# Two small fp32 matmuls per image, each issued as two over the left and right 64 columns

## The chip, the cores and the metric

The kernel runs on one core of one Trainium2 chip. The metric is the device time of one execution in microseconds (us), as the median of several executions. TensorE appears in the profile as two rows: PE for the matmuls and PEld for the loads of their stationary operand (the weights). DVE is VectorE, ACT is ScalarE, POOL is GpSimd, SP is the engine that issues most of the transfers.

## The reference

The input x has 16 images of 32 channels and 96 x 96 pixels. Each channel of each image is normalised (mean 0, variance 1 over its pixels) to v. The means of v over the pixels go through a small gate of seven outputs and a softmax. Each image then gets its own two 3 x 3 kernels as a mixture of seven experts:

```
pooled = v.mean(axis=(-2, -1))
gate   = softmax(pooled @ gate_w.T + gate_b)
kw1    = einsum('be,eoihw->boihw', gate, experts_w1) + conv1_w      # kw2 and both biases alike
out    = x + v + conv(relu(conv(v, kw1) + kb1), kw2) + kb2
```

All of it is fp32. The small matmuls on the way to the gate are fp32 in the kernel as well.

## The kernel before

**Tiling.** An image lies on all 128 partitions: partition group g (of G = 4, 32 channels each) holds the rows 4b + g, in NB = 24 blocks b. A convolution is a sum of matmuls with 128 rows (4 image rows x 32 channels) and 64 columns (2 output rows x 32 channels). It comes in two sides: one fills PSUM partitions 0 to 63 and the other 64 to 127, each through its own half of the array's columns. One side reads the image tile (a1, a2), the other a copy in which the partition halves are swapped (c1, c2). fp32 accuracy comes from fp16 pairs: three products (high x high, high x low, low x high), each over three horizontal taps. So one group (5 blocks, 480 pixels) is 9 pairs of matmuls, and there are GRP = 5 groups for each of the two convolutions of an image: `products` (L369), which records all 2880 convolution matmuls at line 375.

**The two small matmuls.** `gather_rows` (L355) sums the statistics of the four partition groups: a 128 x 128 matrix `same` times a 128 x 12 tile `triples`, into PSUM `pstat`. `logits` (L362) sums over all partitions with a 128 x 128 matrix of ones times the 128 x 7 tile `gwp`, into `pgate`. Each is one fp32 matmul in the code. In the profile each of them stands as two LDWEIGHTS and two MATMUL, since fp32 is executed in two passes.

**Order of the work.** Nothing is planned at run time: each engine has its own list, written out by hand in a function `slot(s)`, one slot for each image, inside a loop of six slots that runs twice (`schedule`, L235). The slots of the engines are coupled by semaphores.
- PE, slot s: conv1 of image s, groups 0 to 3; `gather_rows` of image s+2; conv1 group 4; conv2 of image s-1, groups 0 and 1; `logits` of image s+2; conv2 groups 2 to 4 (L449 to L461). conv1 group 0 waits for the weights, for the low part of the image, for the crossed copy c1 (a transfer) and for PSUM bank 0, which `finish` of image s-2 frees.
- DVE, slot s: `finish` group 4 of image s-2 (L683, adds the result to the image, out of PSUM), `statistics` (L591), the low parts of the hidden layer (L669), `channel_moments` of image s+2 (L610), which waits for `gather_rows`, seven steps of `mixture` for the weights of image s+1 (L638), `weights` (L658), `finish` groups 0 and 1 of image s-1, `softmax_in` of image s+2 (L621), which waits for `logits`, then `finish` groups 2 and 3.
- POOL: `coefficients` (L836, follows channel_moments), the low part of the next images (L852), the residual (L868).
- ACT: normalisation, the hidden layer out of PSUM (L521), the crossed copy for conv2 (L538).
- SP, slot s: load of image s+2 (four transfers, L273), the crossed copy c1 of image s (two transfers, L300), then the stores of image s-2: four transfers after `finish` group 2 and four after `finish` group 4 (L287). These are in one queue and are issued in this order.

Of the kernel before, what the change touches and what calls it, by code (L numbers as in the profile page):

```python
# [35 lines left out]
P = 128  # L36
# [54 lines left out]
def build(nc, x, w1, b1, w2, b2, ew1, eb1, ew2, eb2, gw, gb, out):  # L91
    N, C, H, W = x.shape
    E = ew1.shape[0]
    G = P // C
# [15 lines left out]
    with ctx:  # L110
        def sb(name, shape, dt=F32):
            return ctx.enter_context(nc.sbuf_tensor(name, shape, dt))

        def sem(name):
            return ctx.enter_context(nc.semaphore(name))
# [21 lines left out]
        same = sb("same", [P, P])  # L137
        row = sb("row", [P, 2, G])
        triples = [sb(f"triples{i}", [P, G, 3]) for i in range(2)]
        ones = sb("ones", [P, P])  # L140
# [8 lines left out]
        gwp = [sb(f"gwp{i}", [P, E]) for i in range(RING)]  # L149
# [6 lines left out]
        pstat = ctx.enter_context(nc.psum_tensor("pstat", [P, 512], F32))  # L156
        pgate = ctx.enter_context(nc.psum_tensor("pgate", [P, 512], F32))
# [21 lines left out]
        rows_ps = sem("rows_ps")  # L179
# [6 lines left out]
        gate_ps = sem("gate_ps")  # L186
# [132 lines left out]
        def _(pe):  # L319
# [35 lines left out]
            def gather_rows(t):  # L355

                pe.wait_ge(mv_ok, t.number + 1)
                nc.tensor.matmul(pstat[:, 0:3 * G], same[:, :],  # L358
                                 triples[t.parity][:, :, :].rearrange("p g a -> p (g a)"),
                                 start=True, stop=True).then_inc(rows_ps, 1)  # L360

            def logits(t):  # L362
                pe.wait_ge(gwp_ok, t.number + 1)
                if not t.known(0):
                    pe.wait_ge(logit_ok, t.number)
                nc.tensor.matmul(pgate[:, 0:E], ones[:, :], gwp[t.ring][:, :],
                                 start=True, stop=True).then_inc(gate_ps, 1)

            def products(v, s, g, pairs, *sides):  # L369
                for image, weight in pairs:  # L370
# [62 lines left out]
            for n in range(8):  # L433
                transpose_kernels(n)
            gather_rows(Sample(0, 0))
            transpose_table()
            logits(Sample(0, 0))
            gather_rows(Sample(0, 1))
            logits(Sample(0, 1))
            warm_up()  # L440
            first_conv1()
            conv1_group(Sample(0, 1), 0)
            gather_rows(Sample(0, 2))
            conv1_group(Sample(0, 1), 1)
            conv1_group(Sample(0, 1), 2)
            conv1_group(Sample(0, 1), 3)
            logits(Sample(0, 2))

            def slot(s):  # L449
# [462 lines left out]
```

## Time and profile before

| | us |
|---|---|
| median of 3 runs | 372.83 |
| lowest, highest | 371.85, 376.41 |
| time of the profiled execution | 373.65 |
| its span, first to last instruction | 371.8 |
| PE busy | 320.5 (86%) |
| DVE busy | 301.0 (81%) |
| ACT busy | 252.6 (68%) |
| POOL busy | 199.6 (54%) |

The span is that of the profiled execution; the 1.85 us between it and the time lie outside the first and last instruction. A busy PE is not PE at its peak, since the matmuls overlap: a matmul of the convolution lasts 0.37 us in the record, but two sides run at once and a new pair starts every 0.20 us. The mean granted TensorE clock was 0.97 of full speed. DMA moved 58.19 MB, mean 157 GB/s.

### The profile page before, as it was taken

The page shows a single profiled execution, that of the slowest core. Times are in us where ns is not written, and L with a number is a line of the kernel's source. Part 1 is how long each engine was busy: PE and PEld are TensorE (multiplying, and loading weights), DVE is VectorE, ACT ScalarE, POOL GpSimd, SP SyncE. Part 2 cuts the span into 40 slices and gives each one's busy share as a digit, 9 for nine tenths or more (in the row PEclk, how much of TensorE's full clock was granted, in tenths as well). Part 3 has the DMA queues.
Part 4 walks back from the last instruction along what each step waited for, and adds up shares of the span by engine and source line. Part 5 has one row for each costly group of instructions (what it writes and reads, how often), then busy time and mean ns, then how long its engine had stood idle before and what let it go on. Part 6 is the DMA issues. An engine that isn't in the chain of part 4 may idle for free.

```text
span 371.8 us, 8541 instructions
## 1 busy us (share of the span) xinstructions
PE 320.5 (86%) x2983; PEld 198.4 (53%) x2983; DVE 301.0 (81%) x679; ACT 252.6 (68%) x278; POOL 199.6 (54%) x236
## 2 busy tenths in 40 slices
PE   2328773599999997999997999989999999999994
PEld 2216532356465754565554557555556555676552
DVE  3699945699979998899988799998999898796432
ACT  1155229877877887797877578887778787866720
POOL 8039417492928484666648084847576674933000
PEclk9999968599999999999999899999999999999999
DMA  9942990607989596949795795969697967194055
GB/s 194 219 74 56 229 189 2 130 3 189 198 191 194 136 234 151 219 116 220 168 203 127 175 194 150 220 150 230 147 203 165 213 148 178 42 216 112 18 130 127
DMA packets 107148, 58.19 MB, mean 157 GB/s; under 512 B 102497, under 2 KB 103009, under 8 KB 107105
## 3 DMA queue, kind: packets, MB, share of 16 engines
q1 hardware_dynamic: 106304, 57.03, 72.3%
q10 hardware_dynamic: 608, 0.59, 0.6%
q8 instruction: 26, 0.43, 0.5%
q14 instruction: 18, 0.14, 0.1%
q0 software_dynamic: 192, 0.01, 0.0%
HBM read 19.47 MB, written 18.87 MB: 103 GB/s over the span
## 4 chain that ended last, share of the span: by engine, by line
PE 38%; DVE 26%; DMA 11%; issue 9%; SPq 9%; ACT 3%; POOL 2%; ACTq 0%; DVEq 0%; POOLq 0%
PE pg L375 36%; DMA c<-a 10%; DVE mix L645 6%; DVE a L672 5%; DVE img L688 4%; SPq L273 4%; SPq L287 3%; DVE wts L662 3%; DVE stats L600 2%; SPq L300 2%; PE pg L338 2%; POOL a L858 1%; DMA natural<-in_L_conv_conv_w 1%; PE pstat L358 1%; DVE wts L665 1%
## 5 line engine op out<-in xcount | busy, mean ns | idle before, releaser
L375 PE MATMUL pg<-a,wts 128*64 128x480 f16 (+1 forms) x1440 | 295.2, 364 | 15.1 <-DMA c<-a 9.2
L375 PE MATMUL pg<-c,wts 128*64 128x480 f16 (+1 forms) x1440 | 300.7, 369 | 0.0
L375 PEld LDWEIGHTS pg<-c,wts 128*64 128x64 f16 x1440 | 155.3, 110 | 72.6 <-issue 1.1
L375 PEld LDWEIGHTS pg<-a,wts 128*64 128x64 f16 x1440 | 155.8, 110 | 52.1 <-issue 15.3
L858 POOL TENSOR_TENSOR a<-xh,a 128x576 f16<-128x576 f32 x64 | 85.3, 1364 | 12.9 <-POOL col L866 8.5
L533 ACT ACTIVATE hid<-pg,col 128x480 f32<-128x480 f32 x80 | 52.4, 656 | 40.8 <-PE pg L375 26.1
L549 ACT COPY c<-a 64x2352 f32<-64x2352 f32 x32 | 68.9, 2153 | 16.3 <-DVE a L672 13.2
L645 DVE SCALAR_TENSOR_TENSOR mix<-bank,gate,mix 128x386 f32<-128x386 f32 x96 | 74.0, 771 | 2.4
L839 POOL TENSOR_TENSOR col<-col,minus_half 128x1 f32<-128x1 f32 x16 | 13.5, 845 | 113.6 <-DVE col L618 113.6
L672 DVE TENSOR_TENSOR a<-hid,a 128x480 f16<-128x480 f32 x80 | 55.5, 695 | 20.8 <-ACT a L533 19.1
L872 POOL TENSOR_SCALAR img<-img,col 128x1152 f32<-128x1152 f32 x32 | 58.4, 1834 | 0.1
L688 DVE SCALAR_TENSOR_TENSOR img<-pg,img 128x480 f32<-128x480 f32 (+1 forms) x80 | 47.1, 631 | 12.7 <-PE pg L375 10.2
L533 ACT ACTIVATE a<-pg,col 128x480 f16<-128x480 f32 x80 | 52.6, 657 | 0.0
L600 DVE BATCH_NORM_STATS2 stats<-img 128x6 f32<-128x384 f32 x96 | 45.6, 544 | 0.1
L490 ACT ACTIVATE xh<-img,col 128x2304 f32<-128x2304 f32 x16 | 36.9, 2306 | 10.0 <-POOL col L840 10.0
L495 ACT ACTIVATE a<-img,col 128x2304 f16<-128x2304 f32 (+1 forms) x17 | 37.3, 2194 | 6.5 <-POOL col L840 6.5
L662 DVE TENSOR_TENSOR wts<-mix,wts 128x384 f16<-128x384 f32 x16 | 20.6, 1290 | 0.3 <-ACT wts L518 0.3
L358 PE MATMUL pstat<-triples,same 128*128 128x12 f32 x32 | 6.9, 290 | 15.4 <-DVE triples L607 15.4
L518 ACT CAST wts<-mix 128x384 f16<-128x384 f32 x16 | 8.2, 512 | 16.0 <-DVE mix L645 16.0
L358 PEld LDWEIGHTS pstat<-triples,same 128*128 128x128 f32 x32 | 5.4, 211 | 21.4 <-DVE triples L607 16.0
L665 DVE COPY wts<-wts 64x768 f16<-64x768 f16 x32 | 13.2, 414 | 0.8
L615 DVE COPY col<-pstat 128x1 f32<-128x1 f32 x16 | 2.5, 157 | 13.3 <-PE pstat L358 13.0
(61 smaller groups left out, 146.0 us busy)
## 6 DMA issues: line engine op xcount, KB each, us to landing
c<-a SPq DMA_DIRECT2D x28, 588.0 KB, 8.7
img<-in_x SPq DMA_DIRECT2D x56, 288.0 KB, 5.6
out<-img SPq DMA_DIRECT2D x60, 180.0 KB, 3.0
out<-img SPq DMA_DIRECT2D x60, 108.0 KB, 2.4
c<-a SPq DMA_DIRECT2D x8, 294.0 KB, 5.3
img<-in_x SPq DMA_DIRECT2D x16, 144.0 KB, 5.0
out<-img SPq DMA_DIRECT2D x4, 120.0 KB, 2.1
out<-img SPq DMA_DIRECT2D x8, 60.0 KB, 1.8
```

The source lines that it names most:

```text
L375: last = nc.tensor.matmul(pg[g][side * 64:side * 64 + 64, at:at + nb * W].rearrange("p (b w) -> p b w", w=W), wts[s.c % WSETS][kind][:, v, ...
L490: nc.scalar.activation(xh[t.parity][:, :, :], img[t.ring][:, :, :], ACT.Identity, bias=c[:, NBIAS:NBIAS + 1], scale=c[:, RSTD:RSTD + 1]).t ...
L495: return nc.scalar.activation(a1[t.parity][:, HI, b0:b1, 1:1 + W], img[t.ring][:, b0:b1, :], ACT.Identity, bias=c[:, NBIAS:NBIAS + 1], sca ...
L533: last = nc.scalar.activation(o, pg[g][:, 0:SPG * W].rearrange("p (b w) -> p b w", w=W), ACT.Relu, bias=c[:, B1:B1 + 1], scale=HS / WS)
L549: last = nc.scalar.copy(d, a[:, :, first:first + NB * RP // 2])
L600: last = nc.vector.bn_stats(stats[t.ring][:, j, :], flat[:, j * SC:(j + 1) * SC])
L645: nc.vector.scalar_tensor_tensor(out=mix[:, (e + 1) % 2, :, :], in0=bank[:, e, :, :], scalar=gate[t.ring][:, e:e + 1], in1=bank[:, E, :, : ...
L662: link(nc.vector.tensor_tensor(st[:, :, LO, :], mix[:, E % 2, :, 0:TAPS], st[:, :, HI, :], ALU.subtract))
L672: nc.vector.tensor_tensor(a2[s.parity][:, LO, j0:j1, 1:1 + W], hid[g_parity(s, g)][:, :, :], a2[s.parity][:, HI, j0:j1, 1:1 + W], ALU.subt ...
L688: nc.vector.scalar_tensor_tensor(out=r, in0=pg[g][:, 0:(b1 - b0) * W].rearrange("p (b w) -> p b w", w=W), scalar=1.0 / (WS * HS), in1=r, o ...
L858: last = nc.gpsimd.tensor_tensor(a1[t.parity][:, LO, b0:b1, 1:1 + W], xh[t.parity][:, b0:b1, :], a1[t.parity][:, HI, b0:b1, 1:1 + W], ALU. ...
L872: last = nc.gpsimd.tensor_scalar(img[t.ring][:, b0:b1, :], img[t.ring][:, b0:b1, :], c[:, RS1:RS1 + 1], c[:, RB:RB + 1], ALU.mult, ALU.add)
```

## The change

`gather_rows` and `logits` are each issued as two matmuls: one over columns 0 to 63 of the stationary matrix, writing PSUM partitions 0 to 63, and one over columns 64 to 127, writing partitions 64 to 127. The moving operand, all 128 rows of it, is read by both. The semaphore is raised by the second one alone. The values computed are the same, and nothing else changes.

```diff
             def gather_rows(t):
 
                 pe.wait_ge(mv_ok, t.number + 1)
-                nc.tensor.matmul(pstat[:, 0:3 * G], same[:, :],
-                                 triples[t.parity][:, :, :].rearrange("p g a -> p (g a)"),
-                                 start=True, stop=True).then_inc(rows_ps, 1)
+                for h0, h1 in ((0, P // 2), (P // 2, P)):
+                    last = nc.tensor.matmul(pstat[h0:h1, 0:3 * G], same[:, h0:h1],
+                                            triples[t.parity][:, :, :].rearrange("p g a -> p (g a)"),
+                                            start=True, stop=True)
+                last.then_inc(rows_ps, 1)
 
             def logits(t):
                 pe.wait_ge(gwp_ok, t.number + 1)
                 if not t.known(0):
                     pe.wait_ge(logit_ok, t.number)
-                nc.tensor.matmul(pgate[:, 0:E], ones[:, :], gwp[t.ring][:, :],
-                                 start=True, stop=True).then_inc(gate_ps, 1)
+                for h0, h1 in ((0, P // 2), (P // 2, P)):
+                    last = nc.tensor.matmul(pgate[h0:h1, 0:E], ones[:, h0:h1], gwp[t.ring][:, :],
+                                            start=True, stop=True)
+                last.then_inc(gate_ps, 1)
```

## Rows read from the trace of the kernel before

**Rows 1.** The page: granted clock in 40 slices, and the busy line.
```profile
PEclk9999968599999999999999899999999999999999
PE 320.5 (86%) x2983; PEld 198.4 (53%) x2983; DVE 301.0 (81%) x679; ACT 252.6 (68%) x278; POOL 199.6 (54%) x236
```
**Rows 2.** Stretches by PE slot: length, busy by engine, clock, DMA share, GB/s.
```profile
82.44:103.13 20.69, 19.05 (x189) 11.86 (x183) 19.84 (x48) 17.45 (x19) 13.04 (x15) 1.00 0.82 175
103.13:122.03 18.90, 18.90 (x184) 11.78 (x186) 16.35 (x39) 14.05 (x17) 10.59 (x12) 1.00 0.88 189
122.03:143.26 21.23, 19.05 (x189) 11.88 (x184) 20.33 (x46) 17.82 (x19) 14.61 (x16) 1.00 0.82 177
143.26:162.16 18.90, 18.90 (x185) 11.24 (x186) 15.62 (x38) 13.36 (x17) 9.90 (x12) 1.00 0.85 182
...
244.18:263.62 19.44, 19.06 (x184) 11.16 (x185) 17.17 (x41) 14.89 (x18) 11.43 (x14) 1.00 0.86 185
...
302.77:321.67 18.90, 18.90 (x184) 11.29 (x186) 17.14 (x41) 14.88 (x17) 11.40 (x13) 1.00 0.56 127
321.67:339.64 17.97, 17.97 (x187) 14.07 (x183) 14.49 (x28) 12.34 (x17) 9.61 (x8) 1.00 0.59 136
```
**Rows 3.** Who waited for whom, 82 to 303 us: total, times, longest.
```profile
DVE col L615 <- PE pstat L358: 7.0, 7, 1.2
PE pg L375 <- DVE img L688: 5.5, 4, 2.3
PE pg L375 <- DMA c<-a: 3.9, 4, 2.2
```
**Rows 4.** Chain of waits, 103 to 144 us: start, us, what.
```profile
103.13 7.53 PE pg L375 x71
110.66 0.34 PE pstat L358 x2
...
111.02 0.06 DVE col L615
...
122.01 0.58 DVE img L688
...
122.61 0.04 SPq L287
...
131.03 1.02 SPq L300
...
132.11 10.81 DMA c<-a
142.92 0.34 issue
143.26 0.80 PE pg L375 x6
```
**Rows 5.** PE in order of time around one `logits`: start, us, operation.
```profile
236.84 0.37 PE L375 MATMUL pg<-c,wts 128*64 128x480 f16 x1
...
237.04 0.36 PE L375 MATMUL pg<-c,wts 128*64 128x480 f16 x1
237.05 0.36 PE L375 MATMUL pg<-a,wts 128*64 128x480 f16 x1
237.34 0.39 PE L366 MATMUL pgate<-gwp,ones 128*128 128x7 f32 x2
237.66 0.39 PE L375 MATMUL pg<-c,wts 128*64 128x480 f16 x1
...
237.89 0.37 PE L375 MATMUL pg<-c,wts 128*64 128x480 f16 x1
```
**Rows 6.** The same stretch, the weight loads.
```profile
237.34 0.30 PEld L366 LDWEIGHTS pgate<-gwp,ones 128*128 128x128 f32 x2 [0.39 <-issue]
237.69 0.11 PEld L375 LDWEIGHTS pg<-c,wts 128*64 128x64 f16 x1
```
**Rows 7.** Line 358 after 100 us: ns minimum, median, maximum.
```profile
L358 PEld LDWEIGHTS pstat<-triples,same x22: 186/188/189, 110.6 to 310.3; 128*128 128x128 f32 x22
L358 PE MATMUL pstat<-triples,same x22: 259/270/280, 110.6 to 310.4; 128*128 128x12 f32 x22
```
**Rows 8.** PE in order of time in the first 25 us.
```profile
18.61 0.60 PE L358 MATMUL pstat<-triples,same 128*128 128x12 f32 x2 [4.29 <-DVE triples L607]
23.91 0.60 PE L358 MATMUL pstat<-triples,same 128*128 128x12 f32 x2 [1.62 <-DVE triples L607]
```

## The prediction

> **What bounds the kernel now.** I read the page first. PE is busy for 86% and DVE for 81% of the span, and the granted clock is near full speed in nearly all slices [rows 1]: neither engine is bound on its own, so the order of waits decides. Next I cut the trace at the starts of conv1 group 0, which gives stretches of one PE slot [rows 2]. The shortest slots take 18.90 us with PE busy for all of it. The slot from 321.67 us on, in which neither `gather_rows` nor `logits` runs any more, takes 17.97 us. So the two small matmuls cost PE (18.90 - 17.97) = 0.93 us a slot, 0.46 us each. From 82.44 to 302.77 us there are 11 slots, from the first row to the one at 302.77 [rows 2], 20.03 us on average, 1.13 us more than PE needs: PE-bound slots alternate with slots of up to 21.23 us. The waits say what fills the rest [rows 3]: PE waits 9.4 us in all at group 0 of conv1, in eight slots, and DVE waits 7.0 us for the result of `gather_rows`. The wait put down to DVE's `finish` is doubtful, as other semaphores are tested with it.
>
> The chain of waits shows the cycle [rows 4]. Conv1 groups 0 to 3 start at 103.13 us and take 7.53. `gather_rows` follows, and DVE has it at 111.02. DVE then works to the end of `finish` group 2 at 122.59 (11.57 us). SP then issues eight stores, four loads and the two crossing transfers, until the last one leaves at 132.11 (9.5 us). It lands 10.81 us later, and conv1 group 0 starts at 143.26. That is 40.1 us for **two** slots: 7.53 + 0.36 + 11.57 + 9.5 + 10.81 + 0.34. An image's crossing goes back to the `gather_rows` of two slots before. Two such chains run side by side, one a slot behind the other, and the slot between (122.03 us) starts when PE gets there. So PE's own time per slot counts only where no landing holds it, and on the chain itself stands one `gather_rows` per two slots, and no `logits`.
>
> **What one site costs.** Around a `logits` [rows 5] pairs start every 0.20 us (236.84, 237.04). The first pass of the small matmul starts 0.30 us after the last pair, the next pair 0.62 us after it, and the one after that another 0.23 later. Without the site 0.20 would stand between them, so the site costs 0.42 + 0.03 = 0.45, which agrees with the 0.46 above. Its parts: the weight loads of the two passes end 0.30 after the first begins, and one lasts 0.188 in the record [rows 6, 7], so they begin 0.30 - 0.19 = 0.11 apart. That makes about 0.21 of serial loading of 128 columns. Ahead of it lies 0.30 - 0.20 = 0.10, in which nothing streams. Behind it lies 0.32 - 0.21 = 0.11 until the next pair's loads, and 0.03 until the stream is up. Convolution loads lie under the stream of the pair before: no such hole is between the pairs. These loads do not: the engine empties on both sides, about 0.21 us of the 0.45.
>
> **The change, part by part.**
> - Removed: two passes over 128 columns per site. Added: four passes over 64. If a load goes by columns, four take 4 x 0.053 = 0.21, as now.
> - The stationary shape is now 128*64, as in all convolution work, so the array needs no other division of its columns. No row shows a 64-column fp32 load among convolution pairs, nor whether what empties the engine is the change of shape or the change of type. I bound it. Best: both holes go (0.21), the first load lies under the last pair, and the two halves load side by side: a site costs 0.11, a gain of 0.34. Worst: the holes stay, and each pass of a half waits for the one before as the passes do now, 0.13 apart (0.39 from the first start to the second end, and the second lasts 0.26) [rows 5, 7]. Four instead of two are 0.27 more: a site costs 0.72. Between these I take the row that the new form is nearest to in shape, the convolution pair: holes gone, first load hidden, three loads of 0.053 in series and 0.03 of start. This gives 0.19, a gain of 0.26.
> - The result's delay: now 0.30 + 0.13 + 0.26 = 0.69 us from the last pair to the end of the second pass [rows 5, 7]. Then it is 0.20 (stream) + 0.16 (three loads) + about 0.18 (a pass behind its load: 0.28 - 0.11, [rows 7]) = 0.54. The gain for DVE is 0.15.
> - Semaphore: raised by the second half only. Nothing is queued behind a new wait, for there is none. DVE, POOL and SP keep their lists.
>
> The Trainium skill, "TensorEngine Tiling (Array Packing)", section Key Properties, says that changing the tiling mode, not just the tile, drains TensorE. The holes of 0.10 and 0.11 us agree with that, and by it they would go. The same page, section Instruction Overhead, speaks against the change: about 60 cycles of overhead for every matmul, and no tiling over a dimension that is already small. By it two further passes would add 2 x 25 ns = 0.05 us a site at 2.4 GHz, 1.6 us over 32 sites if all lay on the path.
>
> **The sum**, against the profiled execution's 373.65 us:
> - the cycle of two slots: 11 slots are 5.5 cycles x 0.15 = 0.8 us less. PE-bound slots gain 2 x 0.26 = 0.5 each on PE, but the next conv1 waits for a landing, so that turns into waiting. It is covered by the crossing transfer. If that cover went, it would be worth up to 0.5 a slot more;
> - the slot 302.77 to 321.67, PE-bound, with PE-bound slots behind it to the end: 0.5 us;
> - samples 1 to 3 (49 to 82 us), where some sites are ahead of waiting work: 0.3 us, a third of their six sites' 1.6;
> - the first four sites: PE is idle before them and two passes take 0.60 us [rows 8], at the lower clock. The same columns are loaded: 0, with bounds of -0.4 and +0.5 for the four.
>
> Together 1.6 us: 372.0 against the profiled execution. The median is 0.8 below it, so I predict **371.2 us**.
>
> **Rivals.**
> 1. *PE decides.* Against the waits above, the landing moves as far forward as PE does, because stores, loads and crossings follow sooner. Then the sites count in full: the 28 sites behind the first four x 0.26 = 7.3 us, or 365.5 against the median, 367 with some of it absorbed. For it: half the slots are PE-bound. Against it: the cycle of [rows 4], and the DMA share of 0.82 to 0.88 in these slots [rows 2], so transfers have little room. Chance 0.08.
> 2. *Nothing goes.* The fp32 passes empty the engine by their type, or the shape is not what does it. Loads 0.21 as before, holes as before, perhaps 0.03 for each further pass: +0.06 x (5.5 + 2 + 3) = +0.6. Time 373.4 against the median. Chance 0.25.
> 3. *Slower.* Each half is a serial pair of passes, the second waiting for the first with 0.13 between all four passes: +0.27 a site. PE's slot is 19.4 instead of 18.90, the cycle 0.27 longer. That is 5.5 x 0.27 + 0.54 + about 0.6 in the early stage + 0.5 in the first sites = 3.1 us, or 375.9. It decides as soon as a site costs over 0.45. For it: the small passes are serial today and the two halves read the same moving tile. Against it: convolution pairs through the two halves of the array start 0.01 us apart and share one 0.20 us (237.04 and 237.05) [rows 5]. Chance 0.12.
>
> **How the numbers follow.** The forecast gets 0.52, and 0.03 is left for an odd shift of the transfers either way. The forecast's own range: site gains of 0.11 to 0.34 and the first sites' bounds give 369.5 to 372.5, widened by how runs of one kernel differ (371.85 to 376.41). To reach the rivals, the range is 367.0 to 376.0. It leaves out the full form of rival 1 and half of the odd cases. Within 2%, about what a measurement can tell from no change, means 365.4 to 380.3. Only rival 1 with the best site price lies below: 0.04. Above lies rival 3 with a lost landing besides: 0.02. Within: 0.94.
>
> **What would show it.** Right: around a site in the profile after, four fp32 passes, the next pair about 0.39 us after the last instead of 0.62; PE-bound slots of 18.4 us; DVE waiting less at channel_moments, PE waiting more at conv1 group 0. Rival 2: 0.62 to 0.68 and slots of 18.9. Rival 3: 0.85 or more and slots of 19.4. Rival 1: PE's waits stay at 9.4 us and the period falls with the slot. I am wrong in the steps if the site gets shorter and the two-slot cycle moves by other than 0.15, or if the landing of 10.8 us changes.

## The result, and the profile after

| | before | changed |
|---|---|---|
| median | 373.77 us (4 runs) | 379.49 us (4 runs) |
| ratio, 95% interval | | 1.0123 (1.0073 to 1.0172) |
| profiled execution, its span | 373.65, 371.8 us | 378.82, 377.0 us |

The change makes the kernel about 1.2% **slower**. The forecast was 371.2 us with a range of 367.0 to 376.0, so it is wrong in sign and in range. Here and below, medians are over all executions of a kernel, while ratios leave out the few that ran over 1.5% above its fastest.

The local part of the argument, the price of one small matmul, holds, and the gain is larger than forecast. The page of the changed kernel, parts 1 and 2 (to set beside [rows 1]):

```profile
PE 315.7 (84%) x3047; PEld 219.3 (58%) x3047; DVE 300.7 (80%) x679; ACT 252.3 (67%) x278; POOL 199.7 (53%) x236
PEclk9999987799899998999998899989998999999998
```

PE does less and is busy for a smaller share of a longer span. Behind the first eight slices the granted clock now dips to 0.8 in seven, where before it did in one. One `logits` of the changed kernel, PE in order of time (beside [rows 5]), and line 359, the new `gather_rows`, after 100 us (beside [rows 7]; ns minimum, median, maximum):

```profile
174.01 0.36 PE L379 MATMUL pg<-c,wts 128*64 128x480 f16 x1
174.06 0.36 PE L379 MATMUL pg<-a,wts 128*64 128x480 f16 x1
174.21 0.23 PE L369 MATMUL pgate<-gwp,ones 128*64 128x7 f32 x2
174.26 0.37 PE L379 MATMUL pg<-a,wts 128*64 128x480 f16 x1
174.29 0.37 PE L379 MATMUL pg<-c,wts 128*64 128x480 f16 x1
174.47 0.36 PE L379 MATMUL pg<-a,wts 128*64 128x480 f16 x1
174.50 0.38 PE L379 MATMUL pg<-c,wts 128*64 128x480 f16 x1
174.68 0.23 PE L369 MATMUL pgate<-gwp,ones 128*64 128x7 f32 x2
174.71 0.37 PE L379 MATMUL pg<-c,wts 128*64 128x480 f16 x1
174.76 0.37 PE L379 MATMUL pg<-a,wts 128*64 128x480 f16 x1
```
```profile
L359 PEld LDWEIGHTS pstat<-triples,same x44: 132/135/137, 109.8 to 315.7; 128*64 128x64 f32 x44
L359 PE MATMUL pstat<-triples,same x44: 173/191/206, 110.0 to 315.8; 128*64 128x12 f32 x44
```

The holes on both sides of the small matmul are gone. The c side starts at 174.01, takes both passes of its half at 174.21, and goes on at 174.29. The a side goes on undisturbed and takes its half at 174.68, between 174.47 and 174.76. Each side loses 0.08 to 0.09 us (0.28 or 0.29 between two of its matmuls instead of 0.20), where before the site cost 0.45. The loss is elsewhere. The stretches of one PE slot in the changed kernel (beside [rows 2]; length, busy by engine with counts, mean granted clock, DMA share, GB/s):

```profile
79.75:101.32 21.57, 18.37 (x189) 13.86 (x190) 20.72 (x49) 18.32 (x19) 13.92 (x16) 1.00 0.81 171
101.32:121.10 19.78, 19.78 (x189) 14.22 (x191) 15.44 (x36) 13.10 (x17) 9.63 (x12) 0.91 0.83 177
121.10:141.85 20.75, 18.44 (x190) 13.13 (x187) 19.93 (x48) 17.55 (x19) 14.33 (x15) 1.00 0.82 173
141.85:161.64 19.79, 19.79 (x190) 12.67 (x191) 15.94 (x37) 13.63 (x17) 10.16 (x13) 0.91 0.81 183
...
182.16:204.14 21.98, 18.37 (x188) 12.06 (x189) 18.87 (x41) 16.64 (x18) 13.72 (x15) 1.00 0.80 171
204.14:226.93 22.79, 20.12 (x189) 17.18 (x191) 16.40 (x37) 12.85 (x17) 8.80 (x11) 0.85 0.71 154
```

Two things are new.

**The clock.** The slots that were PE-bound at 18.90 us are PE-bound at 19.78 us and have a mean clock of 0.91. PE waits longer at group 0 of conv1, and behind the wait it runs at the lower level:

```profile
PE pg L379 <- DMA c<-a: 10.4, 4, 3.2
PE pg L379 <- POOL a L862: 3.6, 1, 3.6
PE pg L379 <- issue: 2.7, 1, 2.7
PE pg L379 <- DVE img L692: 2.1, 1, 2.1
```
```profile
91.28 9.80 DMA c<-a
101.32 8.84 PE pg L379 x70
...
131.52 10.09 DMA c<-a
```

The first fence is the waits of PE from 79 to 309 us: 18.8 us in all, of which 6.3 lie at the loop's jump, where [rows 3] had 9.4, of which 2.3 at the jump. The second is the chain of waits of the same kernel from 101 to 142 us. Groups 0 to 3 take 8.84 us behind a wait of 3.2, for 7.53 in [rows 4].

**The loop's jump.** One slot went from 20.69 us (203.27 to 223.96 before) to 22.79. It is the first one of the loop's second lap. PE in order of time there, idle time in brackets:

```profile
204.14 0.52 PE L379 MATMUL pg<-a,wts 128*64 128x384 f16 x1 [3.61 <-POOL a L862]
204.14 0.61 PE L379 MATMUL pg<-c,wts 128*64 128x480 f16 x1
207.43 0.53 PE L379 MATMUL pg<-a,wts 128*64 128x384 f16 x1 [2.67 <-issue]
207.43 0.61 PE L379 MATMUL pg<-c,wts 128*64 128x480 f16 x1
```

After the jump one pair runs, and then PE idles for 2.67 us with nothing to wait for that the profile shows. The kernel before has the first stall (2.25 us at 203.27) and not the second. From the jump to the second stall the trace has 8 records of PE (matmuls, their loads, and the sequencer's own instructions). PE's list has four instructions more for each small matmul (two passes, each with its load). Four images' worth of both sites stand in front of the loop, which is 8 x 4 = 32 instructions. So the theory: PE gets its instructions in blocks, ahead of use while it goes straight on. The change moved the loop's first instruction to 8 before the end of a block, so after the jump the next block is needed at once. Before, 40 were left, enough to cover its arrival. The profile has a sign of such blocks: a queue of its own, `q8 instruction`, moves packets of 0.43 MB / 26 = 16 KB, and one of them falls between 204.2 and 207.4 us, the time of the second stall.

The sequencer's record of the jump says the same of the first stall. The taken branch lasts 3.72 us on PE in the kernel before and 5.03 in the changed one, 0.05 to 0.07 us on the other four engines, and 0.08 on PE where it is not taken (320 us).

**Where the 5.2 us between the two spans lie.** Cut at the starts of conv1 group 0, in us:

| stretch | before | changed | difference |
|---|---|---|---|
| up to the first full slot of [rows 2] | 82.44 | 79.75 | -2.7 |
| five slots ahead of the jump | 99.51 | 102.41 | +2.9 |
| the slot that ends in the jump and the one behind it | 42.01 | 44.77 | +2.8 |
| four slots behind these | 78.81 | 81.35 | +2.5 |
| the rest | 69.03 | 68.72 | -0.3 |

So the loss in the eleven slots, 8.2 us, is partly hidden by an early gain, and only a third of it lies at the jump. The early gain is in the other traces too: kernels with whole small matmuls reach this slot at 81.9 to 82.8 us, kernels with both split and no idle matmuls ahead of it at 79.8 to 81.0. What makes it was not looked into.

### The profile page after: what moved, and what is told of

Its sections match the earlier page's. It is cut to its first block, busy times and chain, and to the rows that moved or that the text cites. A ratio compares the mean times of both kernels' runs of the same rounds, so it can differ in the third digit from the quotient of the medians.

```text
span 377.0 us, 8669 instructions
## 1 busy us (share of the span) xinstructions
PE 315.7 (84%) x3047; PEld 219.3 (58%) x3047; DVE 300.7 (80%) x679; ACT 252.3 (67%) x278; POOL 199.7 (53%) x236
## 4 chain that ended last, share of the span: by engine, by line
PE 35%; DVE 20%; DMA 13%; issue 11%; SPq 11%; POOL 6%; ACT 3%; ACTq 0%; DVEq 0%; POOLq 0%
PE pg L379 33%; DMA c<-a 12%; DVE mix L649 5%; SPq L287 5%; SPq L273 4%; POOL a L862 4%; DVE a L676 3%; DVE img L692 3%; DVE stats L604 2%; SPq L300 2%; DVE wts L666 2%; PE pg L338 1%; DMA natural<-in_L_conv_conv_w 1%; ACT a L499 1%; POOL img L876 1%
## 5 line engine op out<-in xcount | busy, mean ns | idle before, releaser
L379 PE MATMUL pg<-a,wts 128*64 128x480 f16 (+1 forms) x1440 | 299.5, 368 | 24.2 <-DMA c<-a 15.2
L379 PEld LDWEIGHTS pg<-a,wts 128*64 128x64 f16 x1440 | 157.5, 112 | 64.7 <-issue 23.7
L359 PE MATMUL pstat<-triples,same 128*64 128x12 f32 x64 | 7.2, 206 | 16.0 <-DVE triples L611 16.0
L359 PEld LDWEIGHTS pstat<-triples,same 128*64 128x64 f32 x64 | 7.8, 149 | 18.2 <-DVE triples L611 16.6
L369 PEld LDWEIGHTS pgate<-gwp,ones 128*64 128x64 f32 x64 | 7.9, 145 | 9.3 <-POOL gwp L853 7.4
```

What stands on the lines that cost most here:

```text
L379: last = nc.tensor.matmul(pg[g][side * 64:side * 64 + 64, at:at + nb * W].rearrange("p (b w) -> p b w", w=W), wts[s.c % WSETS][kind][:, v, ...
```

## The experiments

Theory C is the clock's share, theory J the jump's, theory S that the split form itself costs. All ratios are to runs of the kernel before on the same chip.

**PE's slot made shorter in another way.**
```diff
+LEFT_OUT = ((HI, LO, 0), (HI, LO, 1), (HI, LO, 2), (LO, HI, 0))[:4]
...
                     for kw in range(3):
+                        if v == 1 and g == 3 and (image, weight, kw) in LEFT_OUT:
+                            continue
```


> The kernel before, both small matmuls whole, but four of the nine pairs of conv2 group 3 are left out (that part of the output is not computed): PE's slot is 4 x 0.204 = 0.8 us shorter, about what the change takes out of it (18.9 to 18.2). Theory C (a shorter PE slot only lengthens the wait at conv1 group 0, the clock falls to 1.2 GHz there in every other slot and group 0 and 1 take 1.6 us longer): no gain in the steady slots although work is gone; slots with a granted clock of 0.91, 376 to 380 us in spite of the last three slots being 0.8 us shorter each. Theory S (the split form itself is the cost, by its passes or by the longer instruction list): nothing of that is here, time 369 to 372, no slot at 0.91 but the one behind the loop's jump.

Measured: 374.2 us, ratio 0.9996 (0.9962 to 1.003). Some 13 us of PE work are gone (16 images x 0.8), and the time is the same. So a shorter PE slot is worth nothing here by itself, which speaks for the cycle in [rows 4]. It is not slower either, so the expectation of theory C, 376 to 380, missed, and so did that of theory S, 369 to 372. Theory C is weakened by this, not out: at the end of the kernel nothing waits, and there the missing pairs must save 0.8 us in each of at least two slots (an estimate, from pairs that start 0.20 us apart), so the slots before have given back some 1.6 us. Four pairs of image 0 stand in front of the loop, so it also starts 16 instructions earlier. Its profiled execution took 379.41 us, far from the median, so no row of it is used.

**Idle matmuls in front of the wait.**
```diff
+            def fillers(s):
+                for _ in range(4):
+                    for side in range(2):
+                        nc.tensor.matmul(pset[side * 64:side * 64 + 64, 0:480], fill[:, 0:64], fill[:, :],
+                                         start=True, stop=True)
...
+                run(fillers, s, 0, 2)
                 run(conv1_group, s, 0, 2, 0)
```


> The changed kernel, with four pairs of idle matmuls (fp16, 128*64 x 480, results never read) in front of the waits of conv1 group 0 in each slot from 2 on: 0.82 us of PE activity that takes the place of part of the wait. Theory C: the idle stretch gets 0.8 us shorter, the clock stays at 2.4 GHz in most slots, 372 to 375 us, with more work on PE. Theory S (the split form itself costs): nothing is given back, PE has 12 x 0.8 us more to do and the instruction list is longer still, 379 to 386 us.

Measured: 376.4 us, ratio 1.0079 (1.0037 to 1.012), between the two expectations; its interval overlaps that of the changed kernel (1.0073 to 1.0172), so no gain is shown. The matmuls also run in the last slots, where PE sets the time: the one from 322.67 us takes 18.81, where that of the changed kernel takes 18.0. PE stalls for 2.64 us a second time behind the jump here too.

**Each half of the change alone.**

> Only gather_rows is split; logits is whole. PE's slot is about 0.37 us shorter (18.5). Theory C: the idle stretch at conv1 group 0 grows by about 0.4 us only, so some but not all of every other slot fall to the lower clock; the gather result is 0.2 us earlier on the chain: 372 to 377 us. Theory S, cost by the split form: half of the change's 5.7 us, 376 to 377, with no more low-clock slots than before.

> Only logits is split; gather_rows is whole. logits stands in the half of PE's slot that ends in the wait, not on the chain. Theory C: as with gather_rows alone, but without its 0.2 us per two slots on the chain, so 1 us slower than that: 373 to 378 us. Theory S: half of the change's loss, 376 to 377.

Measured: `gather_rows` alone 374.01 us, ratio 0.9952 (0.9903 to 1.0002); `logits` alone 376.44 us, ratio 1.0012 (0.9955 to 1.0069). Theory S wanted a ratio of about 1.006 for each half. That of `gather_rows` is out of reach of it, that of `logits` is not, so this pair alone does not settle it. Each puts 16 instructions in front of the loop instead of 32. The trace of the kernel with `gather_rows` alone:

```profile
201.30 0.34 PE L377 MATMUL pg<-a,wts 128*64 128x384 f16 x1 [2.16 <-DVE img L690]
...
202.14 0.37 PE L377 MATMUL pg<-c,wts 128*64 128x480 f16 x1
204.02 0.53 PE L377 MATMUL pg<-a,wts 128*64 128x384 f16 x1 [1.51 <-issue]
```

The second stall is there, later and shorter (1.51 us; 1.71 with `logits` alone). From the jump to it both have 24 records of PE: 16 more than the changed kernel, exactly the instructions that were not added.

**The loop's place moved, without the change and with it.**
```diff
-WARM = 7
+WARM = 11
```
This is the edit of the changed kernel; the kernel before gets 15, and 3 as a control.


> The changed kernel with 11 instead of 7 warm-up matmuls (fp32, ahead of the first convolution, in a wait for a transfer). Each is four instructions, so the loop's first instruction stands 16 places further on in PE's list. Theory J (behind the loop's jump PE executes 8 instructions and then waits 2.67 us for its next block of instructions, since the change put 32 more in front of the loop and the loop now begins 8 before the end of a block): that second stall is gone here, 2.5 to 3.5 us less than the changed kernel, 376 to 377. Theory C alone (only the clock falls behind longer waits): no change, 379.5.

> The kernel before with 15 instead of 7 warm-up matmuls: 32 instructions more in front of the loop, so it begins at the same place of the block as in the changed kernel. Theory J: a second stall of about 2.7 us behind the loop's jump appears in a kernel whose small matmuls are whole, and the time rises by 2.5 to 3.5 us, to 376.5 to 377.5. Theory C alone: as before, 374.1.

> The kernel before with 3 instead of 7 warm-up matmuls: the loop begins 16 instructions earlier in its block, still far enough from the end of it. Control for the two kernels with more warm-up. Theory J: no second stall, same time as before (374, within 0.3%). If the number of warm-up matmuls itself moved the time (a colder start of the first convolution), 1 to 2 us more; then part of what the 11 and 15 warm-ups showed is not the loop's place.

Measured: changed kernel with 11 warm-ups 373.04 us, ratio 0.9977 (0.9937 to 1.0017). The kernel before with 15: 375.97 us, ratio 1.0069 (1.0029 to 1.0108). With 3: 374.22 us, ratio 1.0007 (0.9976 to 1.0039). The kernel before with 15 warm-ups shows the same picture as the changed one:

```profile
204.08 0.52 PE L375 MATMUL pg<-a,wts 128*64 128x384 f16 x1 [2.38 <-DVE img L688]
204.08 0.61 PE L375 MATMUL pg<-c,wts 128*64 128x480 f16 x1
207.07 0.53 PE L375 MATMUL pg<-a,wts 128*64 128x384 f16 x1 [2.39 <-issue]
```

One pair, then 2.39 us. In the kernel before with 3 warm-ups the loop starts 16 instructions earlier, and by theory J the late block should show behind 40 + 16 = 56 records. It does: the 57th record behind the jump comes after a hole, though a short one, and no other idle time stands in that slot:

```profile
207.97 0.36 PE L375 MATMUL pg<-c,wts 128*64 128x480 f16 x1 [0.42 <-issue]
```

In all kernels with a second stall the next block is there 3.2 to 4.2 us after the branch ends (3.5 here), so what is left of the block in front of the jump decides how much of that time has cover. In the changed kernel with 11 warm-ups the second pair comes at once:

```profile
204.14 0.34 PE L379 MATMUL pg<-a,wts 128*64 128x384 f16 x1 [2.33 <-DVE img L692]
204.14 0.39 PE L379 MATMUL pg<-c,wts 128*64 128x480 f16 x1
204.32 0.33 PE L379 MATMUL pg<-a,wts 128*64 128x384 f16 x1
```

The stall of theory J is shown from both sides, and 3 warm-ups in place of 7 leave the time as it was (the control). Its size was forecast less well. The time of the changed kernel fell by 1.4% with the move (1.0115 to 0.9977), some 5 us, where 2.5 to 3.5 and 376 to 377 us were expected; that of the kernel before rose by 0.7% (2.6 us), and its 375.97 lies just under the expected 376.5 to 377.5. The trace of the changed kernel with 11 warm-ups is shorter than that of the changed one by 2.8 us in the two slots around the jump, but also by 3.7 in the four behind them and by 1.7 in the five in front. Why those follow is not shown.

**The loss measured again, and both suspects taken away.** The second kernel has 11 warm-ups and the idle matmuls in the loop's slots alone:
```diff
-WARM = 7
+WARM = 11
...
+                if not isinstance(s.i, int):
+                    fillers(s)
```


> The changed kernel itself, in the same runs as the kernel before and the next one, since four executions of it carry the whole loss. If the loss is the second stall (2.4 to 2.7 us) and the falls of the clock (four in the steady slots, about 1 us each less what the wait would have taken anyway): 377 to 380, ratio 1.007 to 1.016. If the four executions were an outlier: 374 to 376.

> The changed kernel with 11 warm-up matmuls (loop's place moved, no second stall) and the four pairs of idle matmuls in front of conv1 group 0 in the twelve slots of the loop alone. Both suspected costs are away. If the clock has a share of its own in the looped kernel: 369 to 371.5 us, below the 373.0 of the one with the loop moved only. If it has none: 372.5 to 375.

Measured: the changed kernel again 379.17 us, ratio 1.0115 (1.0063 to 1.0167). Its trace stalls twice too (4.06 and 3.12 us). With both suspects away: 370.61 us, ratio 0.9917 (0.9886 to 0.9947). The loss has turned into a gain of some 3 us, though PE has 12 x 0.8 us more to do than in the changed kernel. How much of it is the change's own is not shown, since the kernel before was not run with idle matmuls. The step from the loop's place alone (0.9977) is 0.6%, but the intervals overlap a little.

**Written out, without a loop.**
```diff
-            with eng.Fori(0, LAPS) as i:
...
-            for s in range(first + RING * LAPS, last + 1):
+            for s in range(first, last + 1):
                 slot(Sample(0, s))
```


> The kernel before written out without the loop. Its one stall at the jump (2.25 us, and the low clock behind it) goes: 370 to 373 us. Theory J with a small share for the clock: the changed kernel written out is within 0.5% of this one, on either side. Theory C as the main cause: the changed one stays 1% slower than this one.

> The changed kernel without the loop: all slots are written out, so no engine jumps. Theory J: both stalls of slot 8 (3.6 and 2.67 us) go; what is left against the kernel before written out the same way is the clock's share alone. 371 to 374 us. If the change's loss were in its matmul form, 377 or more would stay.

> The changed kernel written out, with four pairs of idle matmuls (0.82 us) in front of conv1 group 0 in slots 3 to 13. Nothing jumps here, so only the clock is at stake. Theory C (each fall of the clock costs 1.6 us on PE in a slot where PE sets the pace): the low stretches in the steady slots go, 365 to 367 against 367.8. Rival: PE's own length counts as much as what the clock gives back: 368 to 371.

Measured: the kernel before 367.92 us, ratio 0.986 (0.9817 to 0.9904); the changed one 367.77 us, ratio 0.981 (0.9756 to 0.9864); with idle matmuls 365.34 us, ratio 0.9784 (0.9744 to 0.9823). Without the jump the split costs nothing in all. But both kernels came out well under what was expected (370 to 373, and 371 to 374), so writing out takes away more than the stalls: in the kernel before the cycle of two slots is shorter as well, 38.88 us (121.93 to 160.81) for 40.13. This pair therefore does not single out the jump. The split kernel still loses in the steady slots: twelve of them take 236.5 us in its trace and 232.9 in the other, and its earlier start (80.05 for 82.84 us) makes up for most of that. PE waits 13.0 us at group 0 in the changed one and 4.4 us in the other: the work taken out of PE's slot is there again as waiting. The idle matmuls point the way theory C says, but the intervals overlap.

**SP issues the crossing before the load.**
```diff
-                run(load, s, 2, 1)
-                run(cross1, s, 0, 0)
+                if s.at_least(2):
+                    run(cross1, s, 0, 0)
+                    run(load, s, 2, 1)
+                else:
+                    run(load, s, 2, 1)
+                    run(cross1, s, 0, 0)
```


> The kernel before written out, with the same order on SP. Chain theory: the slots become PE-bound at 18.9 us, 12 x 0.6 = 7 us less than the written-out one (368): 360 to 362, and the split then pays what it takes out of PE's slot, up to 0.7 us a slot: the changed kernel is 3 to 8 us faster in this pair. Rival (transfers bound): 366 to 368, and no difference between the two.

> The changed kernel written out, and SP issues the crossing transfers of an image ahead of the load of the next but one, instead of behind it (from slot 2 on). Chain theory (two slots are held by PE groups 0 to 3, DVE to finish 2, SP's issues and the landing): 3.3 us of issues leave the chain of two slots, PE waits less at group 0, the clock stays up, and PE's 18.2 us or DVE's 18.8 set the slot: 12 slots x 0.7 to 1 = 8 to 12 us less, 356 to 360. Rival (the transfers are the bound, busy 0.81 to 0.88 of the time in these slots): the crossing lands as late as now behind the stores: 366 to 368.

Measured: whole matmuls 361.07 us, ratio 0.9669 (0.9633 to 0.9705); split ones **355.26 us**, ratio 0.9511 (0.9473 to 0.9549), the fastest of all. The slots, first of the kernel with whole matmuls, then of the one with split ones:

```profile
100.87:119.75 18.88, 18.88 (x188) 11.92 (x184) 17.98 (x42) 15.48 (x18) 12.24 (x14) 1.00 0.91 190
119.75:138.63 18.88, 18.88 (x189) 11.94 (x185) 17.98 (x42) 15.47 (x18) 12.24 (x14) 1.00 0.93 191
```
```profile
98.00:116.57 18.57, 18.38 (x190) 11.22 (x189) 17.88 (x42) 15.46 (x18) 12.23 (x14) 1.00 0.91 190
116.57:135.14 18.57, 18.37 (x188) 11.90 (x189) 17.88 (x42) 15.47 (x18) 12.23 (x14) 1.00 0.95 195
```

With whole matmuls PE is busy to the last 0.01 us in each slot, at full clock: the chain through SP is no longer the bound. There the split pays, 1.6% (0.9511 / 0.9669), without overlap of the intervals. In the traces 2.1 us of it are the earlier start, and 3.1 come in the twelve slots. The expected 356 to 360 us were bettered slightly, and those of the first kernel, 360 to 362, were met. DVE is then next: PE waits about 0.2 us a slot for DVE's `finish`, and the chain of waits is DVE's, line after line. The transfers were not the bound at a share of 0.85, since they now run at 0.88 to 0.95.

## Why the prediction was wrong

- **Price of a site: right in kind, too small in size.** Forecast 0.45 to 0.19 us, measured 0.45 to 0.08 or 0.09. PE's slot without a wait is 18.15 us (the changed kernel with 11 warm-ups), 0.75 less than 18.90:

```profile
101.96:120.11 18.15, 18.15 (x188) 13.50 (x189) 15.41 (x35) 13.08 (x17) 9.61 (x12) 1.00 0.90 193
141.11:160.89 19.78, 19.78 (x190) 12.79 (x192) 15.64 (x36) 13.35 (x17) 9.86 (x12) 0.91 0.82 180
```

  By the rule of the Trainium skill, "TensorEngine Tiling (Array Packing)", Key Properties, that a change of tiling mode drains TensorE, the holes had to go; the trace agrees. The same page, section Instruction Overhead, gives about 60 cycles for every matmul, by which a pass would cost 25 ns at 2.4 GHz (an estimate from that figure); here the passes of a half, their loads included, cost 0.08 us for two, and the site got cheaper, not dearer. Rivals 2 and 3, both about this price, are out.
- **The cycle of two slots: right.** Four pairs less per slot change nothing, and SP's order changes 6.85 and 12.5 us (of the written-out kernels).
- **The failed step: "PE-bound slots gain 0.5 each on PE, ... so that turns into waiting. It is covered by the crossing transfer."** The waiting was priced at nothing. Its measured cost is a slot of 19.78 us instead of 18.15, the second row above, where PE pays 1.6 us for the lower clock. Most of that falls on the chain itself: groups 0 to 3, which the sum took over as 7.53 us, now take 8.84. In the cycle, 101.32 to 141.85 is 40.53 us against 40.13, where 0.15 less was forecast. The Trainium skill, "TensorE: Matmul & The Clock Gate", section "HAM oscillation", describes this kind of thing, waits for transfers that let the clock go down in every round; here waits of 2.0, 2.3, 2.9 and 3.2 us were followed by the lower level, and waits of 2.1 us in this kernel and of up to 2.2 us in the kernel before [rows 3] were not. The length of the wait does not decide it alone: the two rows above stand behind waits of 2.62 and 2.60 us, and only the second runs at 0.91. By the table, the nine slots away from the jump lost 5.4 us. In the looped kernel the medians put the clock's share at some 0.6% (373.04 to 370.61 us), with overlapping intervals; it is likely, not shown.
- **What was missing: the loop's jump.** The sum had no term for where the loop's first instruction lies, and no rival had it. By the medians it is the larger part: 0.7% in the kernel before (1.0069), and from 1.0115 to 0.9977, 1.4%, in the changed one. The stall itself is 2.7 us of this; the slot behind it has a mean clock of 0.85 for 0.92 before; the rest is not accounted for. The Trainium skill, "Runtime: NRT & Kernel Launch", section "Instruction fetch mechanics", says that the sequencers stream their lists in blocks and that a taken branch breaks the prefetch and costs a stall. The trace of before agrees with one stall of 2.25 us, and the changed one adds what I did not draw from it, that the next block can be late as well. There was a warning in the trace of before: its longest wait put down to DVE [rows 3] lies at 203.27 us, the first slot behind the jump.
- **Terms of the sum that were off the other way, or misread.** Up to the first full slot the sum had 0.3 us (samples 1 to 3) and 0 (first four sites); the trace has 2.7. The 0.3 does not follow from its own words either, a third of 1.6 being 0.5. And the two passes of 0.60 us in [rows 8] were not at the lower clock: from 18.6 to 25 us the granted clock is 1.00. In the trace after, these sites take 0.40.
- **The whole.** With both away the kernel takes 370.61 us against 373.81, 0.8% less, about twice the forecast's 1.6 us. That is no support for the sum: in the profiled executions the eleven steady slots came out 9 us above it, and the early part 2.4 below.

What stays open: how the loss divides between the loop's place and the clock, since the first moved slots away from the jump too; and the early gain. The size of a block of instructions was not measured directly. An estimate: the written-out kernel before has 2 x 2983 records of matmuls and loads and 23 packets in `q8`, about 260 a packet.

## What to carry to other kernels

Before saving work on an engine, ask what it will wait for afterwards. If the answer is a transfer, the saving is a longer pause, and TensorE can come out of a pause at half its clock; shorten the chain that ends the pause first, here the order of issues on SP, and the same edit then pays 1.6%. And a loop has a place in an engine's instruction list: if an edit ahead of it adds instructions, look at the first slot behind the jump before believing that the edit itself was slow; move the loop by a few harmless instructions, or write it out, and measure again.

## What was not expected of the hardware

- A stall of 1.5 to 3.1 us "for nothing" behind a jump, after exactly 8 or 24 records, in five kernels whose loops start 32 or 16 instructions later than that of the kernel before; one of 0.42 us after exactly 56 records at 16 earlier; none in the kernel before itself, or at 48 later.
- PE's taken branch lasted 3.3 to 5.5 us in the looped kernels, that of the other engines 0.05 to 0.07 us.
- The two halves of the columns run independently, also for fp32: the second half of a small matmul started 0.47 us after the first (174.68 and 174.21), with convolution matmuls of the other side in between.
- Two fp32 passes over 64 columns with their loads take 0.08 us beyond the stream of their side. Two over 128 columns, changing the shape of the array, took 0.45.
